# ScalarE's order inside the attention groups: one output copy and one context conversion change places

## The reference, cut to what matters

```
q, k, v = norm(x) @ Wq, norm(x) @ Wk, norm(x) @ Wv;  q, k = rope(q), rope(k)
scores  = q @ k.T / sqrt(32), masked above the diagonal
x = x + (softmax(scores) @ v) @ Wo
q1 = fake_quant(norm(x));  q2 = fake_quant(ctx_4096)       # round(x / s + z), clipped to 0..255
x = x + q1 @ q2                                            # ctx_4096: (2, 1024, 1024)
x = x + fixed_point_linear(norm(x), weight, bias)
```

## Time and profile before

| | |
|---|---|
| times of three runs | 476.97, 480.43, 481.77 us |
| profiled execution | 480.98 us, span 479.1 us |
| PE busy | 441.4 us, 92% of the span |
| VectorE busy | 377.3 us, 79% |
| ScalarE busy | 300.1 us, 63% |
| GpSimd busy | 288.1 us, 60% |
| chain that ended last, shares of the span | PE 54%, DVE 14%, ACT 11%, POOL 11%, issue 5%, DMA 4% |

### The profile page before, as it was taken

How to read it: one execution, slowest core, us unless ns; L and a number is a source line. 1 busy time by engine, 2 the same in 40 slices (tenths; PEclk the granted TensorE clock), 3 DMA queues, 4 the chain that set the end, 5 groups by cost and what they waited for, 6 DMA issues and landing times.

```text
span 479.1 us, 9721 instructions
## 1 busy us (share of the span) xinstructions
PE 441.4 (92%) x3730; PEld 243.4 (51%) x3730; DVE 377.3 (79%) x961; ACT 300.1 (63%) x302; POOL 288.1 (60%) x157
## 2 busy tenths in 40 slices
PE   0899997998999999999999999998998999899896
PEld 0676453554555555555555555555543444446442
DVE  4989873888788888888978899896297568799775
ACT  3586252123787777787778898889745313797633
POOL 5002463143989999999998888888730980707000
PEclk9999998999899999999999999999999999999999
DMA  8563386612041111101153113333087010000044
GB/s 328 179 248 126 115 269 207 212 45 78 28 152 46 47 57 57 55 27 46 48 174 118 45 75 111 114 112 108 25 284 266 23 45 23 1 1 2 2 177 179
DMA packets 21042, 50.93 MB, mean 106 GB/s; under 512 B 4736, under 2 KB 10112, under 8 KB 19712
## 3 DMA queue, kind: packets, MB, share of 16 engines
q1 hardware_dynamic: 19696, 41.79, 25.5%
q10 hardware_dynamic: 1296, 8.45, 5.0%
HBM read 40.67 MB, written 9.44 MB: 105 GB/s over the span
## 4 chain that ended last, share of the span: by engine, by line
PE 54%; DVE 14%; ACT 11%; POOL 11%; issue 5%; DMA 4%; SPq 0%; ACTq 0%; DVEq 0%; POOLq 0%
PE ps L1465 11%; PE ps L1288 9%; PE ps L1371 7%; PE ps L1616 5%; ACT s1reg L566 5%; PE ps L1352 5%; POOL more L1205 4%; PE ps L1333 4%; PE ps L1313 4%; DVE stat L769 3%; POOL s1reg L1205 2%; PE ps L1571 2%; DMA qstack<-in_x 2%; PE ps L1354 2%; DMA rope_scratch<-s1reg 2%
## 5 line engine op out<-in xcount | busy, mean ns | idle before, releaser
L829 DVE CUSTOM_DVE_ANT_0 ps<-ps,causal 128x512 f32<-128x512 f32 (+3 forms) x256 | 120.9, 510 | 19.7 <-PE ps L1333 16.6
L566 ACT ACTIVATE s1reg<-ps 128x1280 f32<-128x1280 f32 x64 | 78.9, 1233 | 44.4 <-PE ps L1354 44.1
L1288 PE MATMUL ps<-xT,wqx 128*128 128x512 f16 x384 | 96.3, 383 | 0.0
L1465 PE MATMUL ps<-wo_reg,xT 128*128 128x512 f16 x384 | 93.0, 379 | 0.0
L1333 PE MATMUL ps<-kreg,qstack 96*128 96x512 f16 (+3 forms) x256 | 61.4, 305 | 5.3 <-DMA qstack<-rope_scratch 3.3
L1352 PE MATMUL ps<-qstack,kreg 98*128 98x512 f16 (+3 forms) x256 | 57.9, 303 | 0.0
L1288 PEld LDWEIGHTS ps<-xT,wqx 128*128 128x128 f16 x384 | 37.2, 98 | 37.3 <-issue 2.1
L1465 PEld LDWEIGHTS ps<-wo_reg,xT 128*128 128x128 f16 x384 | 36.5, 97 | 36.6 <-issue 0.2
L1186 POOL TENSOR_TENSOR s1reg<-s1reg 128x512 f32<-128x512 f32 x11 | 15.9, 1449 | 64.0 <-DVE s1reg L818 63.9
L1205 POOL TENSOR_TENSOR s1reg<-s1reg 128x1280 f16<-128x1280 f32 x19 | 49.8, 2623 | 5.9 <-ACT s1reg L572 5.7
L1205 POOL TENSOR_TENSOR wkv<-s1reg,wkv 128x1280 f16<-128x1280 f32 x18 | 47.2, 2624 | 5.5 <-ACT wkv L572 5.5
(11 more groups left out here) (134 smaller groups left out, 929.4 us busy)
## 6 DMA issues: line engine op xcount, KB each, us to landing
s1reg<-in_weights ACTq DMA_DIRECT2D x8, 1024.0 KB, 5.2
s1reg<-in_ctx SPq DMA_DIRECT2D x16, 512.0 KB, 4.2
qstack<-rope_scratch SPq DMA_DIRECT2D x48, 128.0 KB, 2.6
rope_scratch<-s1reg SPq DMA_DIRECT2D x40, 128.0 KB, 2.2
qstack<-in_x SPq DMA_DIRECT2D x8, 512.0 KB, 5.1
s1reg<-in_x SPq DMA_DIRECT2D x16, 256.0 KB, 3.2
out<-s1reg SPq DMA_DIRECT2D x7, 512.0 KB, 2.7
s1reg<-in_L_ffn_weight SPq DMA_DIRECT2D x5, 512.0 KB, 6.1
```

The source lines that it names most:

```text
L566: nc.scalar.activation(ebuf[:, j % 2, :], st_ps[:, 0:SCORES], ACT.Exp, scale=EXP_SCALE, bias=P_LOG_SCALE).then_inc(e_done, 1)
L829: last = nc.vector.tensor_tensor_reduce(part, part, causal[:, T - w:T], 1.0, LOWEST, ALU.add, ALU.max, mt[:, G % 2, h, qt:qt + 1])
L1288: last = mm(out_ap, w(ws, k), xT[:, xs, KT * b + k, :], start=(k == 0 and n == 0), stop=(k == KT - 1 and n == 2))
L1465: last = mm(ps[:, bank, :], xT[:, os, KT * b + k, t], wo_sb[:, ws, 4 * h:4 * h + 4, k, :], start=(k == 0 and n == 0), stop=(k == KT - 1 an ...
```

## The change

Two calls change places in ScalarE's list, and nothing else. `ot_high(G-1)`, which stood between the third and the fourth head, now stands behind the fourth head (groups 1 to 14). The first conversion of context rows, which stood between the second head and the third, now stands in front of the first exponential of the group (groups 9 to 14). The second conversion stays at the group's end. The lists of the other engines are as they were.

```diff
                 if g == 0:
                     act.wait_ge(par_ready, 1)
+                if 1 <= g < KV - 1:
+                    ctx(g * 2 - 2, 0, g * 16)
                 exp(G, 0)
                 p_high(G, 0)
                 exp(G, 1)
                 p_high(G, 1)
-                if 1 <= g < KV - 1:
-                    ctx(g * 2 - 2, 0, g * 16)
                 if G <= KV:
                     rope_high(G + 11)
                 exp(G, 2)
                 p_high(G, 2)
+                exp(G, 3)
+                p_high(G, 3)
                 if 0 < G < NG - 1:
                     ot_high(G - 1)
-                exp(G, 3)
-                p_high(G, 3)
                 if 1 <= g < KV - 1:
                     ctx(g * 2 - 1, 1, g * 16)
```

## The result

The changed kernel took 501.49 us (median of 6 runs, 495.07 to 503.78), the kernel before 480.3 us (6 runs). The ratio is 1.0403, with a 95% interval of 1.0348 to 1.0458: slower by 4%, where 500 us were forecast. The profiled execution of the changed kernel took 499.1 us.

A forecast was written before the change was run, and what follows sets the result against it. The prediction took PE, busy 92% of the span, to bound the kernel. Its terms, -1.0 - 0.3 + 5.1 + 8.9 + 6.6 = +19.3 us, against the median of 480.43 gave 500 us, range 492 to 506.

The forecast's parts named there:

- Part 1: `ot_high` behind the fourth head, groups 1 to 14: PE waits less for GpSimd's last low part; -1.0 and -0.3 us.
- Group 9: ScalarE's moved conversion waits for tile 0, landing 4.8 us after issue, delaying the exponentials PE needs: +5.1 us.
- Groups 10 to 14: ScalarE's moved conversion waits for the context tile queued behind the maxima: +1.78 us each, +8.9 us for five.
- The clock: PE's new idle gaps halve its clock in group 9 and three of the other five: 4 x 1.65 = +6.6 us.
- The price for the load: Context loads land in 3.8 us; the skill's 3.2 us for 512 KB was rejected, since the fastest load took 3.6.
- Faster: Rival: the tile is there, the conversion lies in ScalarE's 1.25 us idle time; 477.6 us, chance 0.05.
- Stalls without the clock: Rival: PE keeps 2.4 GHz in the 2 us gaps, losing it only in group 9; 494.8 us, chance 0.31.

The follow-up runs named there:

- experiment 1: Kernel before with only `ot_high` moved behind the fourth head, the conversion left at its old place: 477.63 us, ratio 0.9939.
- experiment 3: Changed kernel with useless matmuls added on PE between the first `values` stretch and the second head's scores, from group 9 on: 496.66 us, ratio 1.0337.
- experiment 4: Changed kernel with SyncE issuing the slot-0 context tile directly behind the maxima, ahead of the residual tile: 493.93 us, ratio 1.0288.
- experiment 5: Changed kernel with the slot-0 context load for groups 10 to 14 issued early, ahead of the maxima in SyncE's list: 484.03 us, ratio 1.0107.
- experiment 2: Kernel before with only the conversion moved in front of the first exponential, `ot_high` left at its old place: 500.23 us, ratio 1.0427.
- experiment 6: As experiment 5, but group 9's conversion stays between the second and third head: 476.66 us, ratio 0.9956.
- experiment 8: Experiment 1 with GpSimd's rotated low part last up to group 8, maxima ahead of scratch transfers, early context load, conversion in front from group 10: 481.33 us, ratio 1.0054.

## Why the prediction was right

The forecast sum was +19.3 us, the groups show +21.3: waits 15.5, clock 7.0, gains -1.3. That the median lies within 1.5 us of the forecast is partly luck, for the six runs spread over 8.7 us.

- **Part 1, -1.3 us forecast.** Confirmed: -0.9 up to group 7, -0.1 into 8, -0.3 into 15 in the changed kernel. The groups go mostly in turn between 14.06 and 14.33, which fits the forecast that two neighbouring gaps add up to a fixed sum; the sum is 0.36 us in experiment 1 (14.06 + 14.34 less twice 14.02), where 0.46 were forecast. The periods of experiment 1 show the rest of `ot_high`'s worth, 0.3 us in each of groups 10 to 14, which the changed kernel hides behind its waits.
- **Group 9, +5.1 us forecast.** The mechanism was right, the size too small by the landing. The period grew by 8.3 us: tile 0 landed 5.8 us after its issue instead of 4.8 (+1.0), and behind the gap PE ran at half speed. In experiment 3, with the clock kept and the tile at 6.0 us (+1.2), the growth is 20.87 - 14.70 = 6.2, against 5.1 plus 1.2. Tile 0's landing is the term that varies: 4.8 us before and in experiment 4, 5.1 in experiment 5, 5.8 to 6.0 after and in experiments 2 and 3, 4.7 to 6.3 over all traces. Why it varies stays open.
- **Groups 10 to 14, +8.9 us forecast.** The two groups with a kept clock grew by 1.96 and 1.62 us, 1.79 on average, where 1.78 were forecast. That is closer than the parts: a group lasts its landing plus 12.25 us, where the forecast has 16.18 - 3.8 = 12.38, mostly because PE follows the exponential in 0.05 us and not in the 0.15 that I took; the two landings, 4.11 and 3.77, were on average 0.14 longer than the 3.8. With the landings of all five the wait makes 5 x 12.25 + 20.28 - 72.0 = 9.5 us.
- **The clock, +6.6 us forecast for four losses.** Four there were, as forecast in group 9 and three of the other five. Less landing and 12.25, the three of groups 10 to 14 cost 17.74 - 16.14 = 1.60, 17.57 - 15.97 = 1.60 and 18.54 - 17.04 = 1.50 us each, where 1.65 were taken. Group 9's cost 2.3 (22.98 - 5.8 against 20.87 - 6.0 in experiment 3), so this term was too small: 7.0 in all. Group 9 in experiments 4, 2 and 5, columns of the earlier trace rows:

```profile
253.60:257.00 3.40, 2.92 (x12) 1.42 (x12) 0.00 (x0) 2.90 (x3) 1.60 (x1) 0.50 0.00 0
...
250.90:257.60 6.70, 3.36 (x16) 1.56 (x20) 0.37 (x1) 5.25 (x5) 2.04 (x1) 0.50 0.07 28
...
248.80:255.60 6.80, 5.38 (x48) 2.63 (x52) 1.22 (x3) 5.14 (x5) 3.67 (x2) 0.50 0.26 80
```

With the changed kernel's stretch (above, PE busy for 4.72 us) half of PE's busy time at 0.50 is 1.5, 1.7, 2.7 and 2.4 us. Reckoned as for the changed kernel, the loss cost 1.4, 1.6, 2.6 and 2.3 us in these four. So a loss costs half of what PE works at the lower clock, and what lies inside the gap is free; the forecast took 3.3 us of such work, and in the changed kernel's group 9 it was 4.7. That the number of losses came out exactly is luck; which gaps lose the clock isn't the same in every execution (below).
- **The price for the load.** The prediction set the Trainium skill's estimate (DMA: Bandwidth & Descriptors, Anatomy of one DMA) of 3.2 us aside, since 14 loads took 3.6 us or more. In experiment 6 tile 2 leaves alone, with no residual tile near it, and lands in 3.2 us. So this trace agrees with the estimate for a load by itself; the loads of the earlier trace rows go out within 2 us of a 256 KB tile or of each other. The estimate would have been too fast for the sum, as the trace said.
- **The rivals.** *Faster* failed at the point that decided it: the tile was not there, and once it is (experiment 6), the time is 476.66 us, where the rival gave 477.6. *Stalls without the clock* (494.8, with the clock lost in group 9 alone) was not run as such. Experiment 3 keeps the clock in group 9 too and measured 496.66; experiment 4 loses it in group 9 alone, with loads that leave 0.62 us earlier, and measured 493.93.

## What to carry to other kernels

Before moving a step to an engine's earlier idle time, list what the step waits for and find where each of these is queued; the idle time is a cover for the step's work, not for the lateness of its input. When a wait enters an in-order list, price what stands behind it, which here was the exponential that PE needed, not the conversion. And count the clock: PE's gaps cost 15.5 us by the waits themselves and 7.0 more by the clock that four of the six lost.

## What the runs showed of the hardware

- Whether an idle gap of PE loses the clock is not a matter of its length alone. In groups 10 to 14 of the changed kernel gaps of 1.81, 1.99 and 2.89 us lost it, 1.87 and 2.21 did not; in experiment 2 gaps of 1.87 and 2.31 us did, 1.46, 1.66 and 1.70 did not. Elsewhere a gap of 2.30 us lost it (ahead of group 0, from 76.2 us, in experiment 6) and one of 2.92 us at the same place in experiment 8 did not. None of 1.51 us or less in groups 10 to 14 lost it. The gap of 1.73 us in group 0, the same in all traces, lost it in the traces of the kernels before and after and of experiment 5, and not in those of the other experiments, though the programs are the same up to there. In the six runs of the changed kernel the mean granted clock goes from 0.970 to 0.988, and the fastest run, 495.07 us, has the highest. So a kernel with such gaps differs from run to run by its losses.
- From the end of ScalarE's exponential to the matmul that waited for it passed 0.05 us (269.44 to 269.49 in the changed kernel's chain), from GpSimd's low part to PE 0.35.
- A 512 KB load took 3.2 us by itself, and 3.7 to 6.5 us with its neighbours in the changed kernel. As the third load of a row (tile 0, behind two residual tiles) it took 4.7 to 6.3 us in different kernels.
